# Reordering the opening of a two-layer transformer kernel, and moving two LayerNorm steps to GpSimd

## The reference

```
x = x + LN(attention1(LN(x)))        # 16 heads of 8, rotary positions, causal softmax
x = x + LN(layer2(LN(x)))
layer2(x): x = x + attention2(rms(x, w1))   # latent keys (16) + rotary part (32), 16 heads, causal
           return x + experts(rms(x, w2))   # one shared expert and the best 2 of 8
LN(x)    = (x - mean) / sqrt(var + 1e-5)    # over the 128 channels
```

## Time and profile before

| | us |
|---|---|
| median of 3 runs | 644.71 |
| lowest and highest | 642.79, 644.81 |
| profiled execution | 640.79 |
| its span | 638.8 |
| DVE busy | 398.9 (62%) |
| POOL busy | 209.2 (33%) |
| ACT busy | 307.2 (48%) |
| PE busy | 541.8 (85%) |

### The profile page before, as it was taken

One profiled execution on the slowest core, in us unless ns is written; L12 is line 12 of the kernel. 1 busy time (PEld: TensorE's weight loads), 2 busy tenths in 40 slices (PEclk: granted clock), 3 DMA queues, 4 the chain that ended last, 5 costly groups with the idle time before them and its releaser, 6 DMA issues.

```text
span 638.8 us, 9915 instructions
## 1 busy us (share of the span) xinstructions
PE 541.8 (85%) x3538; PEld 300.5 (47%) x3538; DVE 398.9 (62%) x942; ACT 307.2 (48%) x585; POOL 209.2 (33%) x273
## 2 busy tenths in 40 slices
PE   3569989888877997799878998989999998899872
PEld 1424435433444554444435555545575456643632
DVE  6588787667757554566755576756556765435463
ACT  1314666664557643456526545644445532564221
POOL 4372454333625522650442311424231110220011
PEclk9976999999889897799979999999999999999987
DMA  9660214113353450201570122216304120000000
GB/s 227 179 178 13 65 47 151 40 40 104 127 106 84 132 164 21 100 35 66 102 198 36 58 49 51 51 68 150 76 10 96 22 52 2 18 2 1 1 17 16
DMA packets 29488, 47.19 MB, mean 74 GB/s; under 512 B 4608, under 2 KB 15104, under 8 KB 28928
## 3 DMA queue, kind: packets, MB, share of 16 engines
q1 hardware_dynamic: 28480, 46.01, 27.0%
q10 hardware_dynamic: 960, 0.56, 0.4%
HBM read 27.22 MB, written 18.87 MB: 72 GB/s over the span
## 4 chain that ended last, share of the span: by engine, by line
PE 58%; DVE 20%; ACT 6%; issue 5%; POOL 4%; SPq 3%; DMA 3%; POOLq 0%; DVEq 0%; ACTq 0%
PE ps L571 12%; PE ps L528 9%; PE ps L634 8%; DVE NM L1144 6%; PE ps L499 6%; PE ps L496 4%; PE ps L501 4%; PE ps L522 3%; DVE terms L1248 2%; PE ps L756 2%; DVE stats L1128 2%; PE ps L578 2%; PE ps L682 2%; PE ps L617 1%; DVE KS L1401 1%
## 5 line engine op out<-in xcount | busy, mean ns | idle before, releaser
L1144 DVE TENSOR_REDUCE NM<-ps 128x1 f32<-128x512 f32 (+3 forms) x352 | 219.3, 638 | 118.7 <-PE ps L501 111.8
L797 ACT ACTIVATE PG<-ps 128x512 f32<-128x512 f32 x320 | 181.4, 596 | 161.2 <-PE ps L528 94.2
L528 PE MATMUL ps<-QS,K 128*128 128x512 f32 x320 | 119.4, 458 | 0.0
L501 PE MATMUL ps<-maskb,identb 128*128 128x128 bf16 x512 | 111.3, 236 | 0.0
L571 PE MATMUL ps<-PG,V 128*32 128x512 f32 (+3 forms) x1024 | 97.7, 455 | 6.9 <-POOL PG L1090 5.2
L499 PE MATMUL ps<-K,QS 96*128 96x256 f32 (+3 forms) x256 | 84.7, 375 | 15.2 <-DVE NM L1144 14.9
L496 PE MATMUL ps<-KS,QS 96*128 96x256 bf16 (+3 forms) x256 | 74.8, 328 | 20.0 <-DVE NM L1144 18.6
L501 PEld LDWEIGHTS ps<-maskb,identb 128*128 128x128 bf16 x512 | 52.8, 103 | 38.7 <-issue 31.3
L528 PEld LDWEIGHTS ps<-QS,K 128*128 128x128 f32 x320 | 51.9, 196 | 38.8 <-issue 20.3
L522 PE MATMUL ps<-QS,KS 128*128 128x128 bf16 (+3 forms) x256 | 63.9, 312 | 4.7 <-DMA QS<-scr 4.2
L988 POOL TENSOR_TENSOR rstd<-ve,half 128x4 f32<-128x4 f32 x20 | 20.5, 1023 | 139.8 <-DVE ve L1136 104.1
(11 more groups left out here) (159 smaller groups left out, 640.7 us busy)
## 6 DMA issues: line engine op xcount, KB each, us to landing
scr<-QC SPq DMA_DIRECT2D x24, 512.0 KB, 2.8
QS<-scr SPq DMA_DIRECT2D x64, 128.0 KB
scr<-room SPq DMA_DIRECT2D x20, 256.0 KB, 2.5
QS<-scr SPq DMA_DIRECT2D x16, 288.0 KB
KS<-scr SPq DMA_DIRECT2D x16, 288.0 KB
QS<-scr SPq DMA_DIRECT2D x64, 64.0 KB
x<-in_x SPq DMA_DIRECT2D x4, 256.0 KB, 5.2
out_x<-x SPq DMA_DIRECT2D x4, 256.0 KB, 2.3
```

The source lines that it names most:

```text
L501: return pe.matmul(dst[:, P * (k - 1):P * k], identb[:], maskb[:, 0, :], start=False, stop=True)
L528: mm = pe.matmul(bank.rearrange("p (h q) -> p h q", h=HG), keys[:, SEQ[n] % 2, P * j:P * j + P], QS2[:, heads, P * i:P * i + P], start=(ke ...
L797: act.activation(PG[:, n % 2, unit_place(LAYER[n], (u + k) % UNITS), :], ps[:, ST0 + (u + k) % 3, :], ACT.Exp, scale=scale).then_inc(exp_d ...
L1144: dve.tensor_reduce(dst, src, AX.X, ALU.max, negate=True).then_inc(fill_read, 1)
```

## The change

1. The memset of the ones in `KS1` moves from DVE to POOL, as POOL's part of `consts`, behind its `ln1` of batch 0. `load1` waits for its semaphore.
2. The rotary table has a semaphore of its own, so that DVE's copies into `wuv_sb` and PE's projection wait for `wqkv` alone.
3. x of batches 1 to 3 is issued by SP ahead of the twelve other tables.
4. In the order of all engines, `ln1` of batch 1 stands ahead of `parts1` of batch 0 (DVE's moments, no work of POOL), and POOL's scale of it, now stage `ln1s`, between `parts1` and `parts1b` of batch 0.
5. `layer_var` on DVE is a semaphore increment alone; POOL does -mean and variance + EPS ahead of its power, for all 16 normalisations.

```diff
-    plan += [(pre, 0, name, 0, 0) for name in ("ln1", "ln1n", "consts", "x1T", "q1", "k1", "parts1", "parts1b", "v1",
-                                                 "v1c", "store1")]
+    plan += [(pre, 0, name, b, 0) for name, b in (
+        ("ln1", 0), ("ln1n", 0), ("consts", 0), ("x1T", 0), ("q1", 0), ("k1", 0), ("ln1", 1), ("parts1", 0), ("ln1s", 1),
+        ("parts1b", 0), ("v1", 0), ("v1c", 0), ("store1", 0))]
     plan += [(pre, 0, "load1", 0, g) for g in range(G)]
-    plan += row(1, ((pre, 0), "ln1", 0), ((pre, 0), "ln1n", 0)) + row(0, ((pre, 0), "wprod", 0), ((pre, 0), "wturn", 0))
+    plan += row(1, ((pre, 0), "ln1n", 0)) + row(0, ((pre, 0), "wprod", 0), ((pre, 0), "wturn", 0))
...
-            for dst, src in QKV_LOADS:
-                sp.dma_start(dst, src).then_inc(loaded_qkv, 16)
+            sp.dma_start(wqkv_sb[:], wqkv[:, 0:5:2]).then_inc(loaded_qkv, 16)
+            for dst, src in ROPE_LOADS:
+                sp.dma_start(dst, src).then_inc(loaded_rope, 16)
+            for k in range(1, B):
+                sp.dma_start(xs[k][:], x_seq[k]).then_inc(x_loaded, 16)
             for dst, src in LOADS:
                 sp.dma_start(dst, src).then_inc(loaded, 16)
...
-                    sp.wait_ge(consts_ready, CONSTS)
+                    sp.wait_ge(ones_ready, 1)
                     sp.wait_ge(cleared, QUERY_ZEROS)
...
             def power(chain):
+                if chain != 2:
+                    pool.tensor_scalar(nmean[chain][:], mv[chain][:, :, 0], -1.0, None, ALU.mult)
+                    step(pool.tensor_scalar(ve[chain][:], mv[chain][:, :, 1], EPS, None, ALU.add))
                 step(pool.tensor_tensor(rstd[chain][:], ve[chain][:], half[:], ALU.pow))
...
+            def consts(b, _):
+                pool.wait_ge(scale_ready, SCALE_OF["ln1n", 0])
+                pool.wait_ge(consts_ready, STACK_ZEROS)
+                pool.memset(KS1[MROW:P].bitcast(F32), TWO_ONES).then_inc(ones_ready, 1)
+                pool.wait_ge(ones_ready, 1)
+
+            def ln1(b, _):
+                if b != 1:
+                    scale("ln1", 0)(b, 0)
+
+            def ln1s(b, _):
+                scale("ln1", 0)(b, 0)
...
             def layer_var(chain):
-                dve.tensor_scalar(nmean[chain][:], mv[chain][:, :, 0], -1.0, None, ALU.mult)
-                dve.tensor_scalar(ve[chain][:], mv[chain][:, :, 1], EPS, None, ALU.add).then_inc(var_ready, 1)
+                dve.sem_inc(var_ready, 1)
...
-                dve.tensor_copy(maskb[:], masks_sb)
-                dve.wait_ge(loaded_qkv, ALL_QKV)
+                dve.tensor_copy(maskb[:], masks_sb).then_inc(consts_ready, 1)
+                dve.wait_ge(loaded_qkv, 16)
...
-                dve.wait_ge(consts_ready, STACK_ZEROS)
-                dve.memset(KS1[MROW:P].bitcast(F32), TWO_ONES).then_inc(consts_ready, 1)
...
             def q1(b, _):
                 if b == 0:
-                    dve.wait_ge(loaded_qkv, ALL_QKV)
+                    dve.wait_ge(loaded_rope, 16 * len(ROPE_LOADS))
                 rotation_of_pair(BANK0["q1", b, 0], JOB0["q1", b, 0], False, rope1_sb)
```

More of the change, by code:

```diff
@@ L322, in block_program @@
         x0_loaded, wuv_ready = sem("x0_loaded"), sem("wuv_ready")
+        loaded_rope, ones_ready = sem("loaded_rope"), sem("ones_ready")
         loaded_late = sem("loaded_late")
@@ L356, in block_program @@
         FIRST_LOADS = ((ident_sb[:], ident[:]), (masks_sb, masks[:]))
-        QKV_LOADS = [(wqkv_sb[:], wqkv[:, 0:5:2])]
-        QKV_LOADS += [(rope1_sb[2 * H * d + H * s:2 * H * d + H * s + H], rope1[H * d:H * d + H]) for d in range(D1 // 2) for s in range(2)]
+        ROPE_LOADS = [(rope1_sb[2 * H * d + H * s:2 * H * d + H * s + H], rope1[H * d:H * d + H]) for d in range(D1 // 2) for s in range(2)]
         LOADS = ((erow_sb, expert_rows[:]),
@@ L368, in block_program @@
         STORED1 = 16 * 5
-        ALL_FIRST, ALL_QKV, ALL_LOADED = 16 * len(FIRST_LOADS), 16 * len(QKV_LOADS), 16 * (len(LOADS) + len(BLOCK_LOADS))
+        ALL_FIRST, ALL_LOADED = 16 * len(FIRST_LOADS), 16 * (len(LOADS) + len(BLOCK_LOADS))
         STACK_ZEROS, CONSTS, EROW, WCO = 1, 2, 3, 4
@@ L417, in turnmax @@
                                  MP[0:2 * HG, m % 2, :]).then_inc(m_stacked[g], 16)
[L419 to L422, removed]
             def store1(b, _):
@@ L484, in fin @@
                 sp.dma_start(out_seq[b], xs[b][:]).then_inc(out_sent, 16)
-            stream(lambda n, hh: None, dict(turnmax=turnmax, ln1=ln1, store1=store1, load1=load1, qabs=store2("qabs"), ropeB=store2("ropeB"),
+            stream(lambda n, hh: None, dict(turnmax=turnmax, store1=store1, load1=load1, qabs=store2("qabs"), ropeB=store2("ropeB"),
                               load2=load2, experts_in=experts_in, fin=fin))
@@ L637, in q1 @@
                 if b == 0:
-                    pe.wait_ge(loaded_qkv, ALL_QKV)
+                    pe.wait_ge(loaded_qkv, 16)
                     pe.wait_ge(wuv_ready, 2)
@@ L1109, in _ @@
             stream(main, dict(
-                clear2=clear2, ln1=scale("ln1", 0), q1=join_terms("q1", [ALU.add]), k1=join_terms("k1", [ALU.subtract]), parts1=parts1, parts1b=parts1b, v1c=v1c,
+                clear2=clear2, consts=consts, ln1=ln1, ln1s=ln1s, q1=join_terms("q1", [ALU.add]), k1=join_terms("k1", [ALU.subtract]), parts1=parts1, parts1b=parts1b, v1c=v1c,
                 o1y2=scale("o1y2", 1), lna=lna, lna2=lna2, kst=join_terms("kst", [ALU.add]),
```

## The result

| | before | after |
|---|---|---|
| median of the runs, us | 644.02 (20 runs) | 647.42 (20 runs) |
| lowest and highest | 639.67, 648.26 | 644.26, 651.96 |
| profiled execution's span | 638.8 | 644.8 |
| granted clock of it | 0.954 | 0.952 |
| DVE busy | 398.9 | 394.2 |

The change made the kernel slower: the ratio of the times is 1.0059, 95% interval 1.0039 to 1.0079, some 3.8 us (the two medians are 3.4 us apart, a quotient of 1.0053, inside the interval). The forecast was 644.3, range 641.0 to 646.6; the result is outside it. What came is nearest to rival 3.

The account below looks back on a forecast made before the run. The prediction took the first 36 us as one chain without slack, its end set by batch 1's projections on PE. Opening -0.1 and LayerNorm -0.3 gave -0.4 us: 640.4 for the profiled execution, 644.3 for the median, range 641.0 to 646.6.

Parts of the forecast that it names:

- rival 3: All normalisations: the longer LayerNorm chain counts everywhere, 0.22 x 14 outside the opening = +3.1, -0.1: 647.7 us; chance 0.10.
- The ones on POOL: Opening: POOL's memset holds DVE's `xn` after the first passes; the second key product is done at 20.9, +2.1 us.
- The upper end of the bounds: Opening, DVE's `xn` beside POOL's memset: from no cost to waiting out the whole 3.51 us; the whole was taken.
- Batch 1's normalisation earlier: Opening: gets back the 2.1 us lost in front; batch 1's projections end at 33.75, 0.1 us earlier than now.
- Its data is in near 34, so two PE fills still fit: Opening, batch 0's first stack load: issued at 28.6, landing between 31 and 36.4, with a microsecond of fills before 35.7.
- the hold: Opening: DVE's `xn` waits out POOL's memset of the ones, making the keys 2.1 us later.
- x ahead of the tables: cost nothing: SP's load queue: three x loads pass twelve tables, 1.5 us of issuing; no cost, at most 1.5 us if late.
- The LayerNorm steps: 16 normalisations, two steps on POOL: DVE gains 0.15 at seven places, power loses 0.22 at two; -0.3 us taken.
- The gain of 0.15 for DVE: Each normalisation: DVE freed of two small steps, a gain at seven places on the chain outside the opening.

Follow-up runs that it names:

- e3: Changed kernel with the memset of the ones on DVE again, behind its copies into `wuv_sb`; ratio to the kernel before 1.0014.
- e4: Changed kernel with the ones still on POOL, but behind DVE's copies into `wuv_sb`; ratio to the kernel before 1.0025.
- e2: Changed kernel with the LayerNorm steps back on DVE, so the opening's four edits alone; ratio to the kernel before 1.0023.
- e14: Changed kernel, with SP waiting for batch 0's first pair of stack loads before issuing the second; ratio to the kernel before 1.0035.
- e5: Changed kernel with the ones on POOL behind DVE's copies and the LayerNorm steps back on DVE; ratio to the kernel before 0.9966.
- e6: e5 with POOL's scale of batch 1 behind the last split of batch 0's queries; ratio to the kernel before 0.9941, 639.98 us.
- e7: e6 with POOL's four clears of the second layer's query stack moved into the opening; ratio to the kernel before 0.9951.
- e1: Kernel before with only the LayerNorm steps moved to POOL, for all 16 normalisations; ratio to the kernel before 1.0050.
- e8: e1 with POOL's two small LayerNorm steps done twice at each normalisation; ratio to the kernel before 1.0099.
- e9: e7, with SP waiting for batch 0's first pair of stack loads before issuing the second; ratio to the kernel before 0.9966.
- e10: Kernel before with only POOL's four clears of the second layer's query stack moved into the opening; ratio to the kernel before 0.9993.
- e12: e6 with x of batches 1 to 3 issued behind the twelve tables again; ratio to the kernel before 1.0015.
- e13: e7 with x of batches 1 to 3 issued behind the twelve tables again; ratio to the kernel before 1.0001.
- e15: e6, with SP waiting for batch 0's first pair of stack loads before issuing the second; ratio to the kernel before 0.9952.

## Why the prediction was wrong

**The ones on POOL: right, to 0.1 us.** First `xn` free, three held: end forecast 13.35, measured 13.26; projections from 15.25, measured 15.27; keys at 20.9, measured 20.95. The upper end of the bounds was the right choice. The Trainium skill's rule ("SBUF — State Buffer", section "Who interferes with whom") was cited for it; e3 and e4 agree with it, as `xn` takes 1.11 us as soon as no POOL instruction lies beside it.

**Batch 1's normalisation earlier: right for PE, wrong for what bounds.** The second projections were put at 29.95 to 33.75 and ran 29.79 to 33.57. The first stack load was put at 28.6 and went at 29.11 (25.80 in the earlier trace rows). The inserted scale was put at 23.1 to 24.9 and ran 23.15 to 25.84; the last split ended at 26.95 and not at 26.1. Half a microsecond of it is POOL's `nmean`, 0.77 us instead of 0.25 beside DVE's `terms` (23.15 and 23.13), and 0.23 the product at 25.41 (0.43 for 0.20): one engine held by the other, which the prediction used in its first step and did not look for in its second.

**"Its data is in near 34, so two PE fills still fit": failed.** The data were in at 36.58, over the upper bound of 36.4, and the first scores started at 36.72 and not at 33.6. In the trace of before the data were in by 33.60 and nobody waited, so no row had their landing; I took a value inside the bounds near the one that cost nothing. By the forecast's own numbers it held only for a landing before 34.7 (35.7 less the microsecond of the two fills), in the middle of bounds from 31 to 36.4. Two things make it large. The stack store is late by the hold (2.1 us) and by POOL's inserted scale, of which edit 5 is a microsecond (e2), and the first pair shares its transfer engines with the three others: 6.5 us with them, 4.8 without (e14). With it, the opening cost +1.6 us at the first `rec` against the forecast of -0.1. In e14 0.85 of this is back, and in e3 and e4, without the hold, all of it and more.

**"x ahead of the tables: cost nothing": right here, by the cover that the hold gave.** The changed kernel waits for no table. Once the hold is gone (e5 to e7) PE's weight product waits 1.5 to 1.9 us for the last one.

**The LayerNorm steps: failed, in the size and in the count, and this is the larger part.** Size: +0.22 to +0.24 per power forecast, +0.40 measured, and +0.61 at the one that POOL reaches late. POOL's two instructions were taken at a spacing of 0.15 from two `tensor_tensor` rows; these `tensor_scalar` and the power behind them stand 0.31 apart each. Count: two powers on the chain were counted, from the chain of before; five are on it after. A chain of waits shows who was last, not by how little. In the kernel before ACT already stood idle for POOL ahead of its `xn` at 71.10, 0.51 us (shown with e1), though the chain went past it through DVE; the longer step moved the chain over. A look at the readers of each normalisation would have shown half of it: outside the opening ACT waited for POOL's scale at four of them (71.10, 135.70, 608.11, 633.10), and in the changed kernel at seven, because at three more the reader had less than the added step in hand. The place in stretch 5, where a POOL instruction moved onto a DVE one, is on no such list.

Forecast -0.3. The stretches at full clock alone give +1.8. In the tail both powers (612.56 and 637.74) are on the chain, +0.40 each, and with like clocks that is the whole difference: 46.18 in e3 (with edit 5) at 0.87 against 45.38 before at 0.88, with 13.02, 24.62 and 7.04 around the two steps against 13.01, 24.63 and 7.03. Together +2.6 us; e1 measured 0.50% (3.2 us, 1.7 to 4.8). The gain of 0.15 for DVE was real, but in one full-clock stretch only (4).

**Rival 3** said +3.1 for a step of 0.22 at all of fourteen places, -0.1 for the opening, and 647.7 in all; the median is 647.42. It was right in kind, and near in size by luck: the step was 0.40, at fewer places, its opening left out a loss that e2 measured at 0.23% (1.5 us), and it was counted from 644.71 where the 20 runs of before have 644.02. I gave it 0.10, with the argument that only two powers were on the chain, which is the argument that failed. e8 ties the loss to the step: a second dose costs about as much as the first.

**Left open.** Why the gains ahead of the first `rec` don't come out in the medians. Behind it the ten kernels without edit 5 (before, e2, e5 to e7, e9, e10, e12, e13, e15) have nearly the same work, alike to 0.05 us in nearly every stretch at full clock, and yet took 565.3 to 572.5 us from one profiled execution to the next, nearly all of the difference in the stretches with a lower clock. 12 runs a kernel give medians to about 0.25%. For the same reason it isn't settled which of e6, e7, e9 and e15 is best. All four are faster than both kernels except that e9's interval touches no change; e6, at 0.9941, has the lowest ratio and the fewest edits of the four.

## What to carry to other kernels

- A chain of waits names the last of several that were nearly late. Before lengthening a step, count all its readers that already wait for it, however briefly, and those that have less in hand than the step adds, and not only those on the chain.
- When work is brought forward in an opening, ask for each transfer that nobody waited for how long it really takes. Its landing is then the next bound, and the loads behind it in the queue are part of its time.
- Moving an instruction to an idle engine is not free where the engines exclude each other: place it (here behind the copies) before counting it as hidden. And whatever lengthens one of the two engines' work moves its next instructions against the other's, as in stretch 5.

## What the hardware showed that I had not expected

- POOL's two small steps start 0.31 us apart (71.18, 71.49), though neither reads the other's result, and the power another 0.31 later (71.80); on DVE the same two started 0.07 to 0.08 apart. Two such steps cost 0.15 us on DVE and 0.62 on POOL.
- A DVE instruction that took 0.15 us before took 0.55 with the same operands, because POOL's work ended 0.6 us later against it, and POOL's `nmean` took 0.77 instead of 0.25 beside DVE's `terms`: each engine was held by the other.
- The first pair of stack loads (288 KB each) was in 4.8 us behind its second issue when alone (e14), and 6.5 us with three more pairs issued behind it: later issues of one queue slow down an earlier one.
- e10: the work of PE between 36 and 50 us took 12.49 us at a granted clock of 0.50 and 9.99 at 0.67, which took back most of what DVE had won there.
